# Adding expert rows to the output in memory instead of reading them back

## The reference

```
x = x + 0.5 * ffn(layernorm(x))      # mixture of 8 experts, the best 2 per token
x = x + attention(layernorm(x))      # causal convolution, 8 heads, blocks of 128 tokens
x = x + 0.5 * ffn(layernorm(x))      # the same experts again

ffn(h):  probs = softmax(h @ router.T); the two largest, scaled to a sum of 1, are c1, c2
         y_e = (silu(h @ gate_e.T) * (h @ up_e.T)) @ down_e.T      # width 176
         out = c1 * y_e1 + c2 * y_e2
```

## Time and profile before

| what | value |
|---|---|
| median of three runs | 756.17 us (756.01 to 756.23) |
| the profiled execution's own time | 758.16 us |
| its span, first to last instruction | 756.4 us |
| PE busy | 664.9 us, 88% |
| DVE / ACT / POOL busy | 520.7 / 491.3 / 372.7 us |
| bytes moved by DMA | 85.50 MB |

### The profile page before, as it was taken

The page is one execution under the profiler, slowest core; times in us unless marked ns, Lnnn a source line. Parts: engine busy times, 40 slices in busy tenths (PEclk is TensorE's granted clock), DMA queues, the critical chain, the costliest instruction groups (busy, mean ns, idle before and its releaser), DMA issues. The chain is left out here.

```text
span 756.4 us, 18879 instructions
## 1 busy us (share of the span) xinstructions
PE 664.9 (88%) x5168; PEld 590.6 (78%) x5169; DVE 520.7 (69%) x1829; ACT 491.3 (65%) x1702; POOL 372.7 (49%) x418
## 2 busy tenths in 40 slices
PE   3999799999996699999898989978778999999854
PEld 3986699999993577878787878767557899999743
DVE  6588466666666467787878777858657677777653
ACT  5775566666664278887877868768444566666633
POOL 4200544444424546657787877554545444444500
PEclk9999899999999789999999999999879999999968
DMA  9930345444442211111222221110224543443289
GB/s 307 304 128 10 106 141 151 143 126 133 129 111 83 77 36 36 50 42 52 77 64 64 71 72 60 33 58 22 88 89 122 160 134 120 130 127 125 71 315 351
DMA packets 60424, 85.50 MB, mean 113 GB/s; under 512 B 10032, under 2 KB 46387, under 8 KB 60340
## 3 DMA queue, kind: packets, MB, share of 16 engines
q1 hardware_dynamic: 47332, 49.73, 21.2%
q0 software_dynamic: 13008, 34.69, 14.6%
HBM read 45.77 MB, written 37.44 MB: 110 GB/s over the span
## 5 line engine op out<-in xcount | busy, mean ns | idle before, releaser
L1811 PE MATMUL CC<-w_hi,turned_parts 128*128 x568 | 175.5, 351 | 3.6 <-issue 3.6
L725 POOL DMA_INDIRECT shared<-h_rows,tok_i x71 | 70.2, 988 | 116.4 <-issue 58.9
L1811 PEld LDWEIGHTS CC<-w_hi,turned_parts 128*128 128x128 f32 x568 | 105.4, 193 | 4.4 <-issue 4.3
L742 POOL DMA_INDIRECT y_rows<-shared,y_dest x71 | 70.0, 986 | 76.0 <-DVE y_dest L1349 57.8
L818 ACT ACTIVATE shared<-CC 128x176 f32<-128x176 f32 x142 | 45.2, 319 | 76.1 <-PE CC L1811 70.1
L1811 PE MATMUL CC<-w_lo,turned_parts 128*128 x284 | 93.3, 328 | 0.0
L934 ACT ACTIVATE pr<-SS,nmax 128x128 f32<-128x128 f32 x256 | 90.5, 401 | 0.5 <-DVE nmax L1542 0.5
L758 POOL TENSOR_TENSOR pr<-pr,prec 128x1024 f32<-128x1024 f32 x31 | 58.9, 1901 | 51.4 <-DVE prec L1572 50.2
L789 POOL DMA_INDIRECT h_regions<-h_store,dest x64 | 65.4, 1022 | 34.9 <-DVE dest L1436 18.4
L1330 DVE TENSOR_TENSOR shared<-shared,CC 128x176 f32<-128x176 f32 x142 | 48.0, 338 | 49.4 <-ACT shared L818 28.0
L766 POOL DMA_INDIRECT yg<-y_rows,slot_i x64 | 62.9, 983 | 34.5 <-DMA y_rows<-shared 15.5
(11 more groups left out here) (376 smaller groups left out, 2100.3 us busy)
## 6 DMA issues: line engine op xcount, KB each, us to landing
yg<-h_regions SPq DMA_DIRECT2D x71, 129.0 KB
y_rows<-shared SPq DMA_DIRECT2D x71, 128.0 KB
w_lo<-y_rows SPq DMA_DIRECT2D x9, 512.0 KB, 8.0
x_sb<-in_x_dram SPq DMA_DIRECT2D x8, 512.0 KB, 8.3
out_dram<-x_sb SPq DMA_DIRECT2D x16, 256.0 KB, 6.2
w_hi<-y_rows SPq DMA_DIRECT2D x7, 512.0 KB, 11.8
w_lo<-in_gupT_dram SPq DMA_DIRECT2D x2, 1408.0 KB, 11.1
shared<-tile_oh SPq DMA_DIRECT2D x32, 64.0 KB
```

What stands on the lines that cost most here:

```text
L725: pool.indirect_dma_start(out=rows[:, s % RING, 0:D], out_offset=None, in_=h_dram[:, :], in_offset=bass.IndirectOffsetOnAxis(ap=tok_i[:, s ...
L742: pool.indirect_dma_start(out=y_dram[0:TOPK * TOKENS, :], out_offset=bass.IndirectOffsetOnAxis(ap=y_dest[:, s:s + 1], axis=0), in_=y_sb[:, ...
L1811: i = pe.matmul(CC[:, 512 * (u % 2):512 * (u % 2) + GU], rows_part[:, u % 2, c * P:(c + 1) * P], weights, start=(n == 1), stop=(n == 3 * DC))
```

## The change

The second layer's results are no longer stored, read back and summed. Instead the attention's result x is stored to the output early, and every tile's rows, scaled by their share, are added to the output in memory by the scatter itself.

- `last_sum` on DVE, ACT and PE, `load_sums`, `store_sums` and the computation of the shares after the last tile are gone.
- SP stores the 16 pairs of tiles of x while attention runs (12 of them) and between the first row loads of the second experts (4).
- A sent row has one value more, the difference of the two best logits. Per tile, ACT computes the rows' shares from it: tanh of half the difference with a sign, then 0.25 * that + 0.25, and uses it as the scale of the copy in line 836.
- SP's load of tile s waits also until the tanh of tile s - 4 is done (`expd`).
- DVE's `y_to` is two operations of one value per partition instead of one.
- The scatter adds into the output. An addition reads and writes the same bytes, so two that may touch the same token are kept apart: scatter s waits always for scatter s - 2; and where tile s has another expert than tile s - 1, also for scatter s - 1. The second wait is against a value read from a table (`drained_i`), which DVE computes with the other tables; where the expert stays the same the value is that of an older scatter. The first scatter waits for the 16 stores.

```diff
@@ sync, load_rows @@
+                        if RING <= s < RING + BEHIND:
+                            store_attended(TILES // 2 - BEHIND + s - RING)
                         if s >= RING:
                             sp.wait_ge(r["rowsT"], s + 1)
                             sp.wait_ge(r["dest"], s - RING + 1)
+                            sp.wait_ge(r["expd"], s - RING + 1)
...
+            def store_attended(g):
+                sp.wait_ge(T["res"], 2 * g + 2)
+                sp.dma_start(out_rows[:, 2 * g:2 * g + 2, :], x_view[:, 2 * g:2 * g + 2, :]).then_inc(written, 16)
...
@@ sync, after the two stores of each pair to `swapped` @@
+                if p >= BEHIND:
+                    store_attended(p - BEHIND)
             load_rows(1)
-            load_sums(1)
-
-            store_sums()
@@ gpsimd, send_sums @@
+                    if s in (RING + 1, EARLY):
+                        pool.wait_ge(T["drain_table"], 1 + s // EARLY)
+                    count = 16
+                    if s > RING:
+                        count = pool.value_load(drained_i[0:1, s:s + 1], min_val=16, max_val=16 * in_ring(0))
                     pool.wait_ge(r["y_sb"], s + 1 + 2)
                     pool.sem_inc(passed_pool, 1)
                     pool.wait_ge(r["dest"], s + 1)
                     pool.sem_inc(passed_pool, 1)
+                    if s == 0:
+                        pool.wait_ge(written, 16 * (TILES // 2))
+                        pool.sem_inc(passed_pool, 1)
+                    if s >= 2:
+                        pool.wait_ge(r[f"st{(s - 2) % RING}"], 16 * ((s - 2) // RING + 1))
+                        pool.sem_inc(passed_pool, 1)
+                    if s >= 1:
+                        pool.wait_ge(r[f"st{(s - 1) % RING}"], count)
+                        pool.sem_inc(passed_pool, 1)
                     pool.indirect_dma_start(
-                        out=y_dram[0:TOPK * TOKENS, :],
-                        out_offset=bass.IndirectOffsetOnAxis(ap=y_dest[:, s:s + 1], axis=0),
-                        in_=y_sb[:, s % RING, :], in_offset=None, bounds_check=TOPK * TOKENS - 1, oob_is_err=False
-                    ).then_inc(r[f"st{s % RING}"], 16)
+                        out=out_flat, out_offset=bass.IndirectOffsetOnAxis(ap=y_dest[:, s:s + 1], axis=0),
+                        in_=y_sb[:, s % RING, :], in_offset=None, bounds_check=TOKENS - 1, oob_is_err=False,
+                        compute_op=ALU.add).then_inc(r[f"st{s % RING}"], 16)
@@ scalar, experts @@
+                def turned_share(u, s):
+                    a.wait_ge(r["dest"], s + 1)
+                    a.activation(share[:, u % RING:u % RING + 1], rows_in[1][:, u % RING, D + 2:D + 3], ACT.Tanh,
+                                 scale=half_sign[:, u % RING:u % RING + 1]).then_inc(r["expd"], 1)
+
+                def share_of(u, s):
+                    of = share[:, u % RING:u % RING + 1]
+                    a.wait_ge(r["expd"], s + 1)
+                    a.activation(of, of, ACT.Copy, scale=0.25, bias=0.25).then_inc(r["scaled"], 1)
...
                     if is_tile(s):
                         silu_s(u % 2, s)
+                        if between:
+                            turned_share(u, s)
                     if is_tile(s - 1):
                         hid_high(u - 1, s - 1)
+                        if between:
+                            share_of(u - 1, s - 1)
                     if is_tile(s - 2):
                         y_s(u - 2, s - 2, j + (u - 2) // RING)
@@ vector, tables and y_to @@
+            def drains(first, end):
+
+                step(v.tensor_tensor(switched[:, first:end], expert_of[0:1, first:end],
+                                     expert_of[0:1, first - 1:end - 1], ALU.not_equal))
+                at = max(first, RING + 1)
+                v.scalar_tensor_tensor(out=drained_i[0:1, at:end], in0=switched[:, at:end], scalar=16.0,
+                                       in1=steps_16[:, at - 1:end - 1], op0=ALU.mult, op1=ALU.add
+                                       ).then_inc(T["drain_table"], 1)
...
-                    v.scalar_tensor_tensor(out=y_dest[:, bass.ds(s, 1)], in0=rows_in[1][:, q, D + 1:D + 2],
-                                           scalar=expert_of[:, bass.ds(s, 1)], in1=rows_in[1][:, q, D:D + 1],
-                                           op0=ALU.not_equal, op1=ALU.add).then_inc(r["dest"], 1)
+                    v.tensor_copy(y_dest[:, bass.ds(s, 1)], rows_in[1][:, q, D:D + 1])
+                    v.tensor_scalar(half_sign[:, q:q + 1], rows_in[1][:, q, D + 1:D + 2],
+                                    expert_of[:, bass.ds(s, 1)], -0.5, ALU.not_equal, ALU.add).then_inc(r["dest"], 1)
@@ vector, scalar, tensor: at the end of each program @@
-            start_shares(R[1])
-            finish_weights(R[1])
-            last_sum()
...
-            difference(R[1])
-            a.wait_ge(R[1]["shares"], 2)
-            last_sum()
...
-            last_sum()
```

More of the change, by code:

```diff
@@ L67 @@
 MASKED = -1e9
+BEHIND = 4
 EARLY = 24
@@ L220, in macaron_kernel @@
         y_dest = sb("y_dest", [P, TABLE_TILES], I32)
+        half_sign = sb("half_sign", [P, RING])
+        share = sb("share", [P, RING])
+        oh_row = oh[0:1, :, :, :].rearrange("p i k e -> p (i k e)")
+        drained_i = oh_row[:, 0:TABLE_TILES].bitcast(I32)
+        steps_16 = oh_row[:, 256:256 + TABLE_TILES]
+        switched = oh_row[:, 384:384 + TABLE_TILES]
         best = sb("best", [P, TILES, E])
@@ L330, in macaron_kernel @@
         for L in range(2):
-            for n in ("shares", "expd", "weights_at", "g0", "g1", "g2", "g3", "rowsT", "rowsT_hi", "rowsT_lo", "gu", "silu",
+            for n in ("shares", "expd", "scaled", "weights_at", "g0", "g1", "g2", "g3", "rowsT", "rowsT_hi", "rowsT_lo", "gu", "silu",
                       "hid", "hidT", "hidT_hi", "hidT_lo",
                       "y", "y_sb", "st0", "st1", "st2", "st3", "dest"):
-                if n not in (("dest",), ("weights_at",))[L]:
+                if n not in (("dest", "scaled"), ("weights_at",))[L]:
                     R[L][n] = sem(f"r{L}_{n}")
@@ L361, in macaron_kernel @@
         x_rows = x.rearrange("b s d -> (b s) d").rearrange("(i p) d -> p i d", p=P)
[L362 removed]
+        out_flat = out.rearrange("b s d -> (b s) d")
+        out_rows = out_flat.rearrange("(i p) d -> p i d", p=P)
         x_view = x_sb[:, :].rearrange("p (i d) -> p i d", d=D)
@@ L396, in low_acc @@
             return (A, B)[at % 2][0:rows_of, 0:width]
[L398 to L418, removed]
         def in_ring(u):
@@ L834, in y_s @@
                     a.wait_ge(r["y"], s + 1 + 2)
-                    after(a, r[f"st{u % RING}"], 16 * round_)
-                    a.activation(y_sb[:, u % RING, :], SS[:, 512 * (u % 2):512 * (u % 2) + D], ACT.Copy
-                                 ).then_inc(r["y_sb"], 1)
+                    y = SS[:, 512 * (u % 2):512 * (u % 2) + D]
+                    if between:
+                        a.wait_ge(r["scaled"], s + 1)
+                        after(a, r[f"st{u % RING}"], 16 * round_)
+                        a.activation(y_sb[:, u % RING, :], y, ACT.Copy, scale=share[:, u % RING:u % RING + 1]
+                                     ).then_inc(r["y_sb"], 1)
+                    else:
+                        after(a, r[f"st{u % RING}"], 16 * round_)
+                        a.activation(y_sb[:, u % RING, :], y, ACT.Copy).then_inc(r["y_sb"], 1)
+                def turned_share(u, s):
[6 more added lines that the diff above has]
+                    a.activation(of, of, ACT.Copy, scale=0.25, bias=0.25).then_inc(r["scaled"], 1)
                 rows_high(0, 0)
@@ L1031, in first_norm @@
                         attention_weights()
[L1033 to L1044, removed]
             def difference(r):
@@ L1112, in add_experts @@
                 v.sem_inc(z["combined"], 1)
-            def last_sum():
-                by_dve = [t for t in range(TILES) if t not in BY_ACT]
-                for pair in zip(by_dve[0::2], by_dve[1::2]):
-                    done = []
-                    for k in range(TOPK):
-                        for n, t in enumerate(pair):
-                            if k == 0:
-                                v.wait_ge(*y_in(t // 2))
-                            else:
-                                v.wait_ge(dve, done[n])
-                            ins = v.scalar_tensor_tensor(out=x_tile(t),
-                                                         in0=y_pairs(t // 2)[:, t % 2, k * D:(k + 1) * D],
-                                                         scalar=wts[:, k, t:t + 1], in1=x_tile(t),
-                                                         op0=ALU.mult, op1=ALU.add)
-                            if k == 0:
-                                st.did(ins)
-                                done.append(st.n)
-                            else:
-                                ins.then_inc(final, 1)
             def step(i):
```

(15 more changed lines are left out.)

35 lines of the change are left out of this document (11 added, 24 removed).

## The result

Four runs of the changed kernel have a median of 793.02 us (789.04 to 795.41), four of the kernel before on the same chip 756.09 us. The ratio is 1.0486, 95% interval 1.0436 to 1.0535: 37 us slower, where 26 us faster was forecast. The profiled execution took 794.8 us, its span 792.7 us.

A forecast was written before the change was run, and what follows sets the result against it. PE's pace, 2.02 us per tile, was taken as the bound before a closing stretch of transfers. Starting at 592.72, 34.5 * 3.9 gives a last scatter at 727.3, plus 3.0 landing 730.3; median 730 us, range 719 to 764.

The forecast's parts named there:

- I take 3.0 us for the transfer: Adding scatter on POOL's queue: transfer taken as 3.0 us, the gather's 2.76 plus a little.
- x: Time from an adding scatter's start to the start of one that waited for it: 3.9 us, 0.9 of it POOL's waking.
- 34.5 intervals: Scatters of tiles 8 to 70: 55 * x/2 plus a whole x at each of 7 expert changes, 34.5 x.
- The upper bound of 4.8: Limit for x from gather plus plain scatter less one descriptor generation, 3.9 us transfer; the lower bound was 3.0.
- rival 2: Scatter chain: x above 4.63 makes the kernel slower, 762 us at 4.8, 776 at 5.2; chance 0.15.
- Break-even: Scatter chain: at x = 4.63 the end reaches the old 756.4 us; beyond it the kernel is slower.
- The first rival: Scatter's addition costs only a second read, 0.4 us: transfer 2.5, x 3.4, PE keeps pace, end 721 us; chance 0.22.
- the lag is made up there. Cost 0: Head: first scatter at 569 to 571 us instead of 567.78; eight scatters in 24.9 us recover it, cost 0.
- Lands 3.0 later: End: last scatter starts at 727.3 us and lands 3.0 later, at 730.3, where the span ends.
- The 36.5 us at the end: End after the last scatter: loads of `y_rows` and sums go, 719.9 instead of 756.4 us, 36.5 less.
- The row loads: SP's loads now wait for tanh: start at 703.6 us, 3.9 available, 2.58 needed; cost 0, 1.3 to spare.
- Rival 3: POOL's register load for the wait starts only after the previous generation: 2.56 us per scatter, end 754 to 763; chance 0.09.

The follow-up runs named there:

- e10: Changed kernel adding into rows of its own in `y_rows`, keeping only the constant wait for the last scatter but one; 1.0009 of the kernel before.
- e2: Changed kernel with its scatter overwriting instead of adding, every wait kept; 0.9958 of the kernel before.
- e8: Changed kernel without the constant wait for the direct forerunner at tiles 1 to 4; 1.0364 of the kernel before.
- e3: Changed kernel with up to three adding scatters under way: constant wait for s - 3, table values for s - 1 and s - 2; 1.0420 of the kernel before.
- e7: Changed kernel with all waits of scatters for scatters removed, adding into rows of its own in `y_rows`; 0.9634 of the kernel before.
- e9: Changed kernel with three adding scatters under way, eight result buffers and no forerunner waits at tiles 1 to 4; 1.0317 of the kernel before.
- e11: e9 with the four last waits for scatter landings on SP's queue instead of POOL's; 1.0307 of the kernel before.
- e6: Changed kernel adding only the first half of each row (512 B), same rows and waits; 1.0287 of the kernel before.
- e1: Kernel before with its scatter to `y_rows` adding instead of overwriting, no waits among scatters; 1.0040 of the kernel before.

## Why the prediction was wrong

Its sum was 730.3 us for the span; 792.7 came. Point by point:

**The step that failed: "I take 3.0 us for the transfer".** It measured 4.07 on average. The waking, 0.9, was right (0.85), so x is 4.9 instead of 3.9. The 62 intervals of the changed kernel, with 12 changes, are 50 * x/2 + 12 * x = 37 x, and 181.8 / 37 = 4.91; e10 gives 5.02 without any change of expert. On the prediction's own 34.5 intervals the size alone costs 34.5 * 1.01 = 34.8 us, and its own formula gives 592.72 + 34.5 * 4.91 + 4.0 = 766: slower already. The upper bound of 4.8 was too low as well, by 0.1 to 0.2. The wrong choice was the value between the bounds. The lower one came from a scatter with the memory to itself, while a plain scatter in this stage takes 3.04 (e2), so the choice "the gather plus a little" was the plain price. The addition adds 1.03 to that, of which 0.57 is POOL's generation. That was named under rival 2 ("POOL may need longer than 0.98 us") but not put into a bound.

The size alone isn't the whole error. Break-even was put at x = 4.63 for 7 changes, no head and nothing behind the last landing. With the head, the 12 changes and the end as measured it lies at (756.4 - 602.48 - 8.4) / 37 = 3.93, so that even the forecast's own 3.9 would have ended at 602.48 + 37 * 3.9 + 8.4 = 755 and gained 1 us. e2, which has that x, measured 0.9958.

The first rival followed the Trainium skill (Collectives: The Full Stack, section The bandwidth ceiling: the add is slow by its two source reads). That section speaks of the adds of a collective between cores, not of a scatter of one core. No run here separates the read from the arithmetic. The second read was priced at 0.4 us; measured is 1.03 for the addition, and what is left of it beside POOL's 0.57 is 0.46. So the price of the read fits, if that rest is the read (not shown); the rival failed by the longer generation, by a plain transfer of 3.04 instead of 2.13, and by the head, the count and the end.

**The count of changes.** 12 instead of 7 among these tiles: 2.5 intervals more, 12.3 us. The words "as long as the expert stays" were applied to an order of tiles that isn't the kernel's. The table's two parts can be read in the code (`EARLY`, `finish_counts`).

**The head.** The first scatter came at 570.5, as forecast (569 to 571) and for the forecast's reason (in e8 POOL's wait before it, to 570.50, ends with a store of x), but "the lag is made up there. Cost 0" failed: tiles 1 to 4 wait by a constant for their forerunners. It cost 9.8 us, of which e8 gets 8.9 back by the medians (8.1 by the distances of tile 8 from tile 0).

**The end.** "Lands 3.0 later" and nothing after it; there are 8.4 us. Up to the last landing it is 3.1 us, then come 5.06 for the drain, which the work behind the scatters used to cover.

These four are 34.8 + 12.3 + 9.8 + 5.4 = 62.3 us, and 730.3 + 62.3 = 792.6 of 792.7. How the 62 intervals split into size and count is a fit by 37 x, borne out by e3 (12 long distances) and e10 (5.02 without them); the third rests on e8; of the last the length is shown, its cause is open.

**What held.** The 36.5 us at the end did go. The row loads aren't late: between 592 and 784 us no wait of PE for a DMA is listed, also with tanh in front of them; in e7, at PE's full pace, between 592 and 700 us, PE waits for one once, 0.9 us, so there is no margin to speak of. ACT's and DVE's additions cost nothing (e7 has them all, and PE is 105.35 of 108 us busy). The tanh takes 0.29 us, and no table load comes with it (each load in ACT's groups occurs once). Rival 3 did not happen with one register load (0.29 us beside the generation), but in a weak form with two (e3). The right branch was rival 2, with a chance of 0.15: the transfer took more than its 3.7 us, and POOL's longer generation was part of it. Its times fell short by the head, the count and the end: even x = 5.2 gave 776.

**A version that is faster.** None that computes everything was found: the best, e9 and e11, are at 1.03. Without the waits (e7) 0.963 would be there, but the twelve changes of expert cost about 12 * (5.0 - 2.0) = 36 us even at PE's pace between them, an estimate from e3's rows, and that eats the 28 us. A table in one part would have 7 changes in all, but its row table would be ready later; this was not tried.

## What to carry to other kernels

An addition in memory turns a stream of independent scatters into a chain: price it as (start to landing, in the busy stage, plus waking) times the number of links, and count the links in the code's real order, with the constants at its start. Take the price of a transfer from the stage where it will run, not from the quiet end, and treat a longer descriptor generation as a bound of its own. When a tail of work goes, look at what it covered: an engine's closing drain counts from then on.

## What the runs showed of the hardware

- A scatter by index with addition takes POOL 1.56 us of generation for 128 rows, without it 0.98; starts are at least 1.86 us apart instead of 1.27. With half the width the generation is still 1.56 us (e6).
- POOL's queue shows 19824 packets instead of 13008, so 6816 = 71 * 96 more. That would fit a packet for each of the 128 rows instead of 32 packets per scatter (an estimate). Against the kernel before, e1 has 8865 packets under 2 KB more and 2049 larger ones less. Its bytes shown are the same, so the read of the destination isn't in them.
- Start to landing 4.07 us on average with addition, 3.04 without, 3.58 with addition and half the bytes (the transfers that the chain of each run lists).
- Additions that don't wait for each other disturb little: the DMA engines' busy share in the stage rose from 0.41 to 0.78 (e1 and e7), and e1, with the additions alone, took 0.4% longer.
- POOL's drain at the end, begun with its transfers landed, took 5.05 to 5.06 us where the last scatters add (the changed kernel, e1 and e7 among them) and 9.3 where they overwrite (the kernel before and e2). Begun before the last adding scatter started, it took 7.6 (e11).
